# An adjacency network on one core: the low half of the support and the bias move to GpSimd, and the end is dealt out anew in halves

## The reference, cut to what matters

```python
def _ggc(x, adj, W, wih, whh, bih, bhh):
    m = adj @ (x @ W)
    gi, gh = m @ wih.T + bih, x @ whh.T + bhh
    r, z = sigmoid(i_r + h_r), sigmoid(i_z + h_z)
    n = tanh(i_n + r * h_n)
    return (1.0 - z) * n + z * x
x = layernorm(x + relu(_ggc(relu(_ggc(x, ...)), ...)))
support = x @ weight
rank = cumsum(adj != 0, axis=1)
k = minimum(deg, 100); pos = rank - (deg - k)
w = mask * where(pos > 0, 0.5 ** (k - pos), 0.0)
x = layernorm(x + w @ support + bias)
```

## Time and profile before

| what | us |
|---|---|
| median of 3 runs | 347.71 (347.25 to 347.92) |
| the profiled execution | 348.46 |
| its span | 346.7 |
| TensorE matmul busy | 329.2 (95%) |
| VectorE busy | 302.2 (87%) |
| ScalarE busy | 185.4 (53%) |
| GpSimd busy | 27.5 (8%) |

### The profile page before, as it was taken

One profiled execution on the slowest core, in us unless ns is written; L12 is line 12 of the kernel. 1 busy time (PEld: TensorE's weight loads), 2 busy tenths in 40 slices (PEclk: granted clock), 3 DMA queues, 4 the chain that ended last, 5 costly groups with the idle time before them and its releaser, 6 DMA issues.

```text
span 346.7 us, 6773 instructions
## 1 busy us (share of the span) xinstructions
PE 329.2 (95%) x2540; PEld 154.3 (45%) x2540; DVE 302.2 (87%) x505; ACT 185.4 (53%) x243; POOL 27.5 (8%) x35
## 2 busy tenths in 40 slices
PE   1998999999999999999999999999999999999992
PEld 0442334333333333333333333545444444789992
DVE  0689879898999999997999678879989999978995
ACT  0203304105122057069458347888797969769983
POOL 2000000000000000000000001000210202013264
PEclk9999999999999999999999999999999999999997
DMA  7999999999999999999998999998999996000002
GB/s 244 414 411 408 409 408 400 384 411 393 372 372 375 366 396 358 328 346 353 317 321 288 384 401 391 353 340 325 366 373 349 364 366 215 11 7 4 2 32 93
DMA packets 32001, 107.86 MB, mean 311 GB/s; under 512 B 3553, under 2 KB 6369, under 8 KB 31969
## 3 DMA queue, kind: packets, MB, share of 16 engines
q1 hardware_dynamic: 31104, 106.15, 81.4%
q10 hardware_dynamic: 864, 1.28, 1.0%
HBM read 106.37 MB, written 1.05 MB: 310 GB/s over the span
## 4 chain that ended last, share of the span: by engine, by line
PE 70%; DMA 10%; ACT 8%; DVE 7%; issue 3%; POOLq 0%; POOL 0%; ACTq 0%; DVEq 0%; SPq 0%
PE m_acc L494 35%; PE out L494 15%; DMA stream<-in_adj_t 9%; PE out L626 6%; PE m_acc L626 4%; PE gate_ps L570 4%; PE gate_ps L577 2%; ACT wexp L806 2%; ACT codes L806 2%; DMA w<-in_w 2%; DVE run L1034 1%; PE gate_ps L599 1%; DVE codes L1179 1%; PE gate_ps L594 1%; ACT mx L766 1%
## 5 line engine op out<-in xcount | busy, mean ns | idle before, releaser
L494 PE MATMUL m_acc<-stream,s_in 128*64 128x512 f32 x488 | 119.2, 596 | 1.3 <-DMA stream<-in_adj_t 1.0
L990 DVE TENSOR_SCALAR codes<-stream 128x1024 uint8<-128x1024 f32 x109 | 72.0, 686 | 6.3 <-DMA stream<-in_adj_t 6.0
L494 PE MATMUL out<-stream,s_mid 128*64 128x512 f32 x264 | 66.3, 593 | 0.0
L494 PEld LDWEIGHTS m_acc<-stream,s_in 128*64 128x64 f32 x488 | 32.9, 137 | 63.6 <-issue 49.2
L494 PE MATMUL m_acc<-stream,s_mid 128*64 128x512 f32 x224 | 51.6, 599 | 0.0
L925 POOL TENSOR_TENSOR rstd<-stat,mhalf 128x4 f32<-128x4 f32 x16 | 24.6, 1535 | 311.7 <-DVE stat L1145 311.7
L1039 DVE SCALAR_TENSOR_TENSOR codes<-codes,run 128x384 uint32<-128x384 uint32 (+2 forms) x62 | 43.9, 709 | 2.1
L1034 DVE TENSOR_TENSOR run<-run,codes 128x768 uint16<-128x768 uint16 (+2 forms) x61 | 42.3, 694 | 2.0
L709 ACT ACTIVATE m_high<-m_acc 64x512 f32<-64x512 f32 x13 | 7.7, 594 | 56.1 <-PE m_acc L494 47.2
L494 PEld LDWEIGHTS out<-stream,s_mid 128*64 128x64 f32 x264 | 18.9, 137 | 37.0 <-issue 36.3
L743 ACT ACTIVATE rz<-gate_ps,b_rz 128x256 f32<-128x256 f32 x32 | 13.4, 468 | 36.8 <-PE gate_ps L577 36.8
(11 more groups left out here) (171 smaller groups left out, 402.3 us busy)
## 6 DMA issues: line engine op xcount, KB each, us to landing
stream<-in_adj_t SPq DMA_DIRECT2D x192, 512.0 KB, 6.1
wexp<-in_adj_t SPq DMA_DIRECT2D x2, 512.0 KB, 5.6
late<-in_adj_t SPq DMA_DIRECT2D x2, 512.0 KB, 6.5
third<-in_x_pairs SPq DMA_DIRECT2D x8, 128.0 KB, 6.3
out_nodes<-stream SPq DMA_DIRECT2D x8, 128.0 KB, 2.0
hx<-in_x_pairs ACTq DMA_DIRECT2D x1, 512.0 KB, 7.5
third<-in_adj_t SPq DMA_DIRECT2D x1, 512.0 KB, 7.8
run<-in_adj_t SPq DMA_DIRECT2D x1, 512.0 KB, 9.7
```

Of the source, the lines that this page charges most:

```text
L494: last = nc.tensor.matmul(to[D * u:D * (u + 1), :], state[:, t * D:(t + 1) * D], data[:, u * CW:(u + 1) * CW], start=start[u], stop=stop)
L990: nc.vector.tensor_scalar(edges(p // 2, b, 2 * (p % 2), 2), loaded(n), 0.0, None, ALU.not_equal).then_inc(mask_made, 1)
```

## The change

Three things change, and nothing before stage 1.

First, `split_low` and `add_bias` of sources 0 to 6 (`BY_POOL = 7`) are on GpSimd, in this order behind the power of their stage; those of source 7 stay on VectorE.

Second, who expands which block, and when. In stage 1 ScalarE's square goes ahead of its first expansion, in stage 3 a third expansion goes ahead of `split_high`, and one chain step of stage 1 (its two operations) moves behind the reduction. Of the last blocks (7,1), (2,6), (3,7) and (7,7) go from VectorE to ScalarE, and (7,4), (6,6) and (2,7) the other way; (4,6) stays on ScalarE, later. VectorE's count goes from 22 to 21, and ScalarE's from 42 to 43.

Third, the end. Output chunks 3, 4 and 5 are scaled by ScalarE (0, 2 and 4 before). The last chunk's blocks of sources 5, 6 and 7 are multiplied in two halves: first the lower half of the nodes of all three, then the upper. The upper half has a bank of its own, that of output chunk 0, so block (0,7) waits for `y_made`. Additions, square, reduction, power, scale and store of the last chunk are done by halves.

```diff
-BY_DVE = [AHEAD[4], AHEAD[6], AHEAD[7], AHEAD[8]] + \
-    [REST[n] for n in (2, 5, 7, 9, 11, 12, 14, 16, 18, 19, 21, 22, 24, 26, 28, 30, 32, 34)]
+    [REST[n] for n in (2, 5, 7, 9, 11)] + \
+    [(6, 5), (7, 3), (7, 4), (7, 5), (0, 6), (3, 6), (5, 6), (6, 6), (7, 6), (1, 7), (2, 7), (5, 7)]
-ACT_EXPANDS = {1: (1, 1, 1), 2: (1, 2, 2), 3: (1, 2, 3), 4: (1, 2, 2), 5: (1, 2, 2),
+ACT_EXPANDS = {1: (0, 2, 1), 2: (1, 2, 2), 3: (1, 3, 2), 4: (1, 2, 2), 5: (1, 2, 2),
-ACT_END = (1, 1, 1, 1, 1, 0, 0, 0)
-DVE_END = (2, 2, 1, 1, 1, 1, 0, 0)
+ACT_END = (1, 1, 2, 1, 1, 0, 0, 0)
+DVE_END = (1, 1, 3, 1, 1, 0, 0)
+DVE_SCALES = {5: (0,), 6: (1, 2)}
-OUT_ACT = (0, 2, 4)
+OUT_ACT = (3, 4, 5)
+LAST = NCH - 1
+SPLIT_FROM = 5
+HALVES = (slice(0, KT // 2), slice(KT // 2, KT))
-CHAIN_CUT = [(1, 2), (2, 4), (2, 3), (2, 3)] + [(1, 2)] * 3 + [(0, 1)] * 2
+CHAIN_CUT = [(1, 2), (1, 3), (2, 3), (2, 3)] + [(1, 2)] * 3 + [(0, 1)] * 2
...
+            def share_last():
+                for part, tiles in enumerate(HALVES):
+                    for j in range(SPLIT_FROM, NCH):
+                        if part == 0:
+                            if (j, LAST) in BY_DVE:
+                                pe.wait_ge(by_dve, BY_DVE.index((j, LAST)) + 1)
+                            else:
+                                pe.wait_ge(by_act, BY_ACT.index((j, LAST)) + 1)
+                        last = share_tiles(j, LAST, range(tiles.start, tiles.stop))
+                    last.then_inc(last_done, 1)
...
+            def split_low(s):
+                pool.wait_ge(sup_high, s + 1)
+                nc.gpsimd.tensor_tensor(support(s)[:, :, 1, :], sup_f, support(s)[:, :, 0, :],
+                                        ALU.subtract).then_inc(sup_made, 1)
             for s in range(NCH):
                 to_rstd(s, 0)
+                if s < BY_POOL:
+                    split_low(s)
+                    add_bias(s)
...
-                add_bias(t - 1)
-                split_low(t - 1)
+                if t > BY_POOL:
+                    add_bias(t - 1)
+                    split_low(t - 1)
...
+            dve.wait_ge(last_done, 1)
+            add_high(LAST, HALVES[0])
+            add_low(LAST, LAST, HALVES[0])
+            sum_squares(NCH + LAST - 1, LAST - 1, ysq[:, LAST - 1])
+            sum_squares(NCH + LAST, LAST, ysq[:, LAST, HALVES[0]], HALVES[0])
+            dve.wait_ge(last_done, 2)
+            add_high(LAST, HALVES[1])
+            add_low(LAST + 1, LAST, HALVES[1])
+            scale_out(LAST - 1, LAST - 1)
+            sum_squares(NCH + LAST + 1, LAST, ysq[:, LAST, HALVES[1]], HALVES[1])
+            scale_out(LAST, LAST, HALVES[0])
+            scale_out(LAST + 1, LAST, HALVES[1])
```

More of the change, by code:

```diff
@@ L298, in build, with end_bank @@
         end_ps = out_ps + [m_acc[0], m_acc[1], n_ps, rz_ps]
+        def end_bank(i, t):
+            return end_ps[0] if i == LAST and t >= KT // 2 else end_ps[i]
         def m2_bank(b):
@@ L414, in build @@
         by_act, by_dve, block_done = sem("by_act"), sem("by_dve"), sem("block_done")
[L415 removed]
+        half_made, y_made, last_done = sem("half_made"), sem("y_made"), sem("last_done")
         o_by_act, o_by_dve = sem("o_by_act"), sem("o_by_dve")
@@ L603, in share @@
             def share(j, i):
-                first, last_j = j == 0, j == NCH - 1
+                first = j == 0
                 pe.wait_ge(sup_made, j + 1)
@@ L622, in share, with share_tiles @@
                         pe.wait_ge(x1_made, NCH)
+                        pe.wait_ge(y_made, 1)
+                share_tiles(j, i, range(KT)).then_inc(block_done, 1)
+            def share_tiles(j, i, tiles):
+                first, last_j = j == 0, j == NCH - 1
                 w, half = weights(j, i), support(j)
-                for t in range(KT):
+                per_bank = KT // 2 if i == LAST else KT
+                for t in tiles:
                     for k in range(KT):
-                        last = nc.tensor.matmul(end_ps[i][:, t * P:(t + 1) * P],
+                        last = nc.tensor.matmul(end_bank(i, t)[:, t * P:(t + 1) * P],
                                                 w[:, k * CW + t * P:k * CW + (t + 1) * P],
-                                                half[:, k, :, :], start=first and t + k == 0,
-                                                stop=last_j and t + k == 2 * KT - 2)
-                last.then_inc(block_done, 1)
+                                                half[:, k, :, :],
+                                                start=first and t % per_bank == 0 and k == 0,
+                                                stop=last_j and (t + 1) % per_bank == 0
+                                                and k == KT - 1)
+                return last
+            def share_last():
[8 more added lines that the diff above has]
+                    last.then_inc(last_done, 1)
             def pass1(b):
@@ L695, in _ @@
                 chunk2(t, FIRST[t])
-            for n in range(RING, len(ORDER)):
+            for n in range(RING, len(ORDER) - (NCH - SPLIT_FROM)):
                 if ORDER[n] in GATES_END:
```

90 lines of the change are left out of this document (58 added, 32 removed).

## The result

| | before | changed |
|---|---|---|
| median of the runs | 347.69 us (4 runs) | 345.3 us (344.8 to 346.18, 4 runs) |
| ratio | | 0.9934 [0.9915, 0.9952], -2.3 us |
| profiled execution: time, span | 348.46, 346.7 | 346.18, 344.1 |
| the rest outside the span | 1.8 | 2.1 |
| busy: TensorE, VectorE, ScalarE, GpSimd | 329.2, 302.2, 185.4, 27.5 us | 328.7, 299.2, 187.6, 47.2 us |

The forecast was 346.2, the measured median is 0.9 lower.

A forecast was written before the change was run, and what follows sets the result against it. TensorE was taken as the bound (70% of the chain), VectorE as second limit. The middle's -0.96 and the end's -0.6 gave -1.6 us: 346.9 profiled, 346.2 for the median, range 345.2 to 349.2.

The forecast's parts named there:

- deciding term: VectorE in stages 3 to 6: two operations leave for GpSimd, 2 x 0.41 - 0.80 = +0.02 us a stage.
- Stage 1: ScalarE's square before an expansion, one chain step moved: make_x1s about 1.1 us earlier, TensorE's 0.43 wait goes; 0.40 taken.
- Stage 3: Third expansion before the high half is free on ScalarE; TensorE's 0.52 us wait at 257.33 goes if VectorE isn't late.
- limit of -1.12: Best possible shift of TensorE up to the last make_x1s: its three waits, 0.40 + 0.52 + 0.20 us.
- R: Reading time each new GpSimd operation costs VectorE: taken as 0.41 us, bounds nothing and 1.01.
- five long powers: GpSimd powers of 1.92 us instead of 1.01 behind two-input chain steps, read as the engines excluding each other while reading.
- Rivals 1: GpSimd holds VectorE longer, which becomes the bound up to the node of 301.86: slower, 350.9 at the upper bound; chance 0.24.
- rival 2: Two sides cancel, VectorE held 0.52 to 0.69 us an operation, middle gives back the end's saving: 347.0 to 348.4; chance 0.24.
- Rival 3: VectorE isn't held at all: TensorE's three waits go (-1.12), the end saves up to 1.1: 345.5 us; chance 0.10.
- forecast's own range: Holding time from 0.3 to 0.52 us and the end from -1.1 to -0.3: 345.5 to 347.2 us; chance 0.42.
- The end: Last chunk finished in halves, VectorE's queue decides: last scale near 343.6 instead of 344.23, -0.6 us, bounds -0.3 and -1.1.
- rival 4: The end saves nothing as three powers queue on GpSimd: the bound of -0.3, moving any case by 0.3; no chance given.

The follow-up runs named there:

- the end alone: Changed kernel with low half and bias back on VectorE and the old order of stages 1 and 3, keeping only the new end: 346.66 us, ratio 0.9965.
- order and end: Changed kernel with all low halves and biases on VectorE (BY_POOL = 0), ScalarE's and the chain's order and the end as changed: 345.71 us, ratio 0.9938.
- kernel without bias: Changed kernel with GpSimd's bias addition of sources 0 to 6, and VectorE's wait for it, left out: 345.77 us, ratio 0.9937.
- the bias twice: Changed kernel with GpSimd's bias addition issued twice for each of seven sources: 347.10 us, ratio 0.9983 to the kernel before.
- tight end without GpSimd: Changed kernel with VectorE's last rows reordered, scales of chunks 1 and 2 put off, low halves and biases all on VectorE: 348.12 us, ratio 1.0011.

## Why the prediction came out as it did

**Overall.** The sign, the two places and most of the mechanism were right, and the gain was forecast too small: 1.6 of the 2.3 us measured. The order and the end carry the timed gain: 0.8 and 1.3 us alone, 2.2 together. GpSimd's part, which I took for the deciding term at a net of nothing, is worth 0.42 to 0.85 us inside the span and less than the runs can tell in the time.

**Stage 1** (forecast -0.40): VectorE's wait of 0.43 is gone in every kernel with this order, and the section is 0.65 shorter where nothing else comes (25.57). In the profile of the changed kernel 0.20 for a DMA came in its place: net -0.22. The profile before couldn't show it behind the longer wait; the end alone did, and order and end lost the whole gain of the section to it. So what stage 1 pays lies between 0 and 0.65 by execution; what makes the DMA late stays open. `split_low` of source 0 ended at 216.62, ahead of its product at 217.14, as worked out.

**Stage 3** (-0.52): the third expansion was free and the wait went. The section from stage 4 to 5 shrank by 0.68, not 0.52, and the section with the wait of 0.20 by 0.36. My limit of -1.12 was a sum of recorded waits, and that step was wrong in size: three recorded waits of 1.15 us are worth 0.65 + 0.68 + 0.36 = 1.69. The reason could have been read. Ahead of the wait of 257.33 stands, in the trace of before:

```profile
255.74 1.07 PE L626 MATMUL out<-codes,wexp 128*128 128x128 f16 x16
```

From start to start these are 1.59 us. In the changed kernel the same two groups start 0.90 apart (255.12 and 256.02), though the first lasts 1.07: groups that follow without a wait overlap by 0.17 in the records. A recorded wait counts from the end of the first, so it is 0.17 short of what goes when the wait goes. The measured -1.27 is the 1.69 less 0.43, which came back ahead of `node` of stage 2 (26.00 for 25.57).

**The deciding term** (R = 0.41, net +0.02 a stage): R is 0.36 and the net -0.23 (15.89 for 16.12). The held operations show as longer ones (1.58 us), not as ones of 1.22 that start late. The removed side was mis-sized: I counted from `add_bias` to the next chain step, 0.80. From `make_x1s` to that step are 0.60 us now and 1.51 with both operations on VectorE (244.29, 245.80 in order and end), 0.91: `add_bias` also waited for `make_x1s` to end, which the chain step needn't. 0.36 + 0.35 - 0.91 = -0.20.

In stage 6, beside expansions, the hold is 0.51 each, and the stage 14.63 for 14.53. The prediction spoke of two-input steps alone. But of its five long powers the fifth stands behind an expansion, which has one input and ran from 312.99 to 314.21 in the trace of before:

```profile
313.15 1.92 POOL L925 TENSOR_TENSOR rstd<-stat,mhalf 128x4 f32<-128x4 f32 x1 [8.21 <-DVE stat L1145]
```

So VectorE was ahead of TensorE at stage 7 by 0.3 us, where I had them together. The kernel without bias shows that nothing more was to be had there, the one with the bias twice that 0.4 more per stage would have cost. And the forecast had no term for the waits for ScalarE that left VectorE with `split_low`: in the tight end without GpSimd it stands 0.92 us for the high half of source 0 (at 216.25), and `n_input` of stage 2 comes 22.20 after that of stage 0, for 21.34 with GpSimd's part. That this lateness is what costs the early `node` of stage 2 there is read from these rows and was not tried by itself.

The Trainium skill's figure (GPSIMD Engine Reference, section 3.1 Elementwise) put the operation at an estimated 0.55 us; alone it takes 0.72 here, and VectorE is held for half of this.

**Rivals 1 to 3.** R stayed under 0.52, so 1 and 2 didn't come; with one operation more (347.10) something like rival 2 did. Rival 3's price, 345.5, was nearer to the measured 345.3 than mine, by the wrong reason: VectorE is held. (The forecast's own range ends by its terms at 347.3, not 347.2.) The Trainium skill's sentence of the whole instruction (SBUF, State Buffer, section SBUF: two separate sides) fits GpSimd's side, whose addition grows from 0.72 to 1.71, but not VectorE's, which loses 0.36.

**The end** (-0.6, bounds -0.3 and -1.1): -0.90. With the end's clock shifted by 301.86 - 300.20 = 1.66, the first half starts at 339.33 (said: 339.3), the second high at 340.64 (340.7), the powers at 340.46 (340.4) and end at 343.01 (near 343.2). The last scale takes 0.29 for half a chunk, where I kept 0.42. So the mechanism stands, and the 0.3 are 0.2 of the powers' end and 0.1 of the scale's size; half-size powers take 0.70 and 0.81, for 0.8 taken, and rival 4 is out. No product at the end waited for an expansion.

**Outside the span** (taken as unchanged): 2.0 for 1.8, which cost 0.2 us and by luck hid as much of the undersized gain. Kernels with GpSimd's part have 1.84 to 2.63, those without it 1.73 to 1.80. This isn't in proportion to GpSimd's work, and what causes it stays open.

## What to carry to other kernels

Work moved to GpSimd should be priced three times: by what it holds VectorE up, by what stood hidden behind the moved operation (a wait for ScalarE here), and by what the time outside the span does. Read what a wait costs from start to start, against a place where the same groups follow without one, and not from the recorded idle time. Before an operation near the end is put off as filler, look at the order in which the stores behind it are issued.

## What the runs showed of the hardware

- A GpSimd addition of 128x256 float32 takes 0.72 us alone, 1.71 beside VectorE's operations of 1.2 us, two-input or expansion, and 2.77 once, in stage 2, beside a one-input uint8 operation of 128x4096, which took 2.65 for 2.29.
- It holds a VectorE chain operation that begins beside it for 0.36 us and an expansion (uint8 to uint16, 128x2048) for 0.51. An operation of VectorE that was under way first isn't held.
- A GpSimd power of 128x2 takes 0.70 and 0.81 us, of 128x4 1.01, and 1.92 behind one chain operation or expansion.
- SyncE issues stores in the program's order, 0.4 to 0.5 us each when they follow one another: a late first one cost 2 us at the end.
- Two groups of 16 float16 matmuls of 128x128 that follow without a wait start 0.90 us apart and are recorded as 1.07 long, so a wait between them costs 0.17 more than its row shows.
- Time outside the span was 1.73 to 1.80 us in the kernels without GpSimd's part and 1.84 to 2.63 in those with it; the cause is open.
